# Attention and mixture layers: value products of two key tiles issued together, at steps 3 and 7 of a slot

## What is computed

```
x = x + A(layernorm(x));  x = x + F(layernorm(x))     # twice, A with other weights

A:  q, k = rotary(x Wq), rotary(x Wk);  v = x Wv      # 16 heads of 8
    y = softmax(causal(q k^T * scale)) v;  return y Wp + bp
F:  q, k = x Wq, x Wk                                 # 8 heads of 64, no mask
    v[h] = sum_e gate_v[h, e] * (x Wv[e])             # the two best of 5 experts
    attn = softmax(q k^T / 8) v
    return sum_e mask_o[h, e] * attn[h] Wo[e]         # the two best of 5 experts
```

## Time and profile before

| what | value |
|---|---|
| median of 3 runs | 2078.11 us (2077.97 to 2079.36) |
| the profiled execution's own time | 2074.39 us |
| its span, first to last instruction | 2072.6 us |
| mean granted TensorE clock over the span | 0.967 of full speed |
| busy: TensorE, VectorE, ScalarE, GpSimd | 88%, 76%, 61%, 51% |

### The profile page before, as it was taken

One profiled execution on the slowest core, in us unless ns is written; L12 is line 12 of the kernel. 1 busy time (PEld: TensorE's weight loads), 2 busy tenths in 40 slices (PEclk: granted clock), 3 DMA queues, 4 the chain that ended last, 5 costly groups with the idle time before them and its releaser, 6 DMA issues.

```text
span 2072.6 us, 32651 instructions
## 1 busy us (share of the span) xinstructions
PE 1816.3 (88%) x11328; PEld 881.0 (43%) x11328; DVE 1580.1 (76%) x2934; ACT 1273.3 (61%) x2803; POOL 1047.0 (51%) x1124
## 2 busy tenths in 40 slices
PE   1658999989999898989999998999999899998775
PEld 0223443535444353535444453544435354443332
DVE  4538787888878788788888888887878888787461
ACT  0335757576675757566675756667575766758461
POOL 1223556363645646374655636465563636455433
PEclk8879999999999999999999999999999999999986
DMA  3231203112121302113120211213021121200000
GB/s 97 48 36 32 37 29 43 35 26 30 37 37 42 36 30 33 23 37 36 42 37 30 40 33 27 33 39 37 29 44 35 26 29 37 36 17 14 11 1 6
DMA packets 87617, 68.71 MB, mean 33 GB/s; under 512 B 10720, under 2 KB 83104, under 8 KB 87328
## 3 DMA queue, kind: packets, MB, share of 16 engines
q1 hardware_dynamic: 87456, 66.62, 17.5%
HBM read 32.51 MB, written 10.49 MB: 21 GB/s over the span
## 4 chain that ended last, share of the span: by engine, by line
PE 64%; DVE 13%; ACT 10%; POOL 6%; DMA 3%; issue 3%; SPq 0%; POOLq 0%; DVEq 0%; ACTq 0%; PEldq 0%
PE Y L463 11%; PE M L556 5%; POOL Z L1069 5%; PE S2a L428 5%; ACT Pq L683 5%; PE S1c L404 5%; PE S2b L428 4%; DVE nmaxF L848 4%; PE M L593 3%; PE S1b L404 3%; PE M L514 3%; PE M L489 3%; DMA Ks<-parts 3%; DVE ztmp L930 3%; PE Y L454 2%
## 5 line engine op out<-in xcount | busy, mean ns | idle before, releaser
L1069 POOL TENSOR_TENSOR Z<-Z,ztmp 128x1280 f32<-128x1280 f32 x112 | 324.5, 2897 | 327.9 <-DVE ztmp L958 326.8
L1036 POOL TENSOR_SCALAR_AFFINE_SELECT PT<-PT 128x256 f32<-128x256 f32 (+1 forms) x640 | 254.5, 409 | 386.6 <-ACT PT L668 383.5
L1060 POOL TENSOR_TENSOR Vf<-Vf,ztmp 128x512 f32<-128x512 f32 x256 | 349.0, 1363 | 102.2 <-DVE ztmp L930 93.6
L668 ACT ACTIVATE PT<-S2a 128x512 f32<-128x512 f32 x320 | 191.6, 599 | 170.6 <-PE S2a L422 166.2
L463 PE MATMUL Y<-PT,Vf 128*64 128x512 f32 x1024 | 274.8, 617 | 0.0
L672 ACT ACTIVATE PT<-S2a 128x512 f32<-128x512 f32 x256 | 153.6, 600 | 158.5 <-PE S2a L428 155.7
L930 DVE TENSOR_TENSOR ztmp<-xv,wv_s 128x512 f32<-128x512 f32 x256 | 238.0, 930 | 2.8 <-POOL Z L1069 2.8
L404 PE MATMUL S1c<-Kf,Qf 64*128 64x512 f32 x352 | 203.6, 659 | 36.2 <-ACT Pq L683 32.2
L404 PE MATMUL S1a<-Kf,Qf 64*128 64x512 f32 x352 | 204.5, 662 | 20.6 <-ACT Pq L683 20.6
L668 ACT ACTIVATE PT<-S2b 128x512 f32<-128x512 f32 x320 | 191.5, 598 | 26.3 <-PE S2b L422 26.0
L404 PE MATMUL S1b<-Kf,Qf 64*128 64x512 f32 x320 | 182.8, 652 | 9.5 <-ACT Pq L683 9.5
(11 more groups left out here) (108 smaller groups left out, 3760.7 us busy)
## 6 DMA issues: line engine op xcount, KB each, us to landing
Qs<-parts SPq DMA_DIRECT2D x96, 128.0 KB
Ks<-parts SPq DMA_DIRECT2D x96, 128.0 KB
tab_s<-in_tab SPq DMA_DIRECT2D x16, 512.0 KB, 4.5
xr<-out_x SPq DMA_DIRECT2D x32, 256.0 KB, 2.9
out_x<-res SPq DMA_DIRECT2D x32, 256.0 KB, 2.2
wa_s<-in_wa SPq DMA_DIRECT2D x16, 320.0 KB, 3.1
xl<-out_x SPq DMA_DIRECT2D x16, 256.0 KB, 3.0
out_x<-in_x SPq DMA_DIRECT2D x8, 256.0 KB, 4.4
```

The source lines that it names most:

```text
L668: nc.scalar.activation(PT[:, slot % 2, b, :], t[:, :], ACT.Exp, scale=SCALE_A).then_inc(exps_done.sem, 1)
L1036: last = nc.gpsimd.affine_select(out=v, in_=v, compare_op=ALU.is_ge, fill=0.0, base=0, pattern=pattern, channel_multiplier=-1)
L1060: nc.gpsimd.tensor_tensor(Vf[:, i, :, :], Vf[:, i, :, :], vtmp[:, n % VBUF, :, :], ALU.add).then_inc(v_acc.sem, 1)
L1069: nc.gpsimd.tensor_tensor(Z[:, :, :, :], Z[:, :, :, :], ztmp[:, hh % 2, :, :, :], ALU.add).then_inc(z_acc.sem, 1)
```

## The change

The value products of kt 0 and 1 are both issued at step 3, those of kt 2 and 3 both at step 7; steps 1 and 5 issue none. Nothing else differs: the same instructions, in another place of TensorE's order.

```diff
                         if b < N_BANKS[slot]:
                             pass2(slot, b)
-                        if b % 2 == 1 and b < 2 * NT:
+                        if b in (3, 7):
+                            values(slot, b // 2 - 1)
                             values(slot, b // 2)
                         at = (slot, b)
```

## The result

The change made the kernel slower: a median of 2089.74 us (5 runs, 2089.01 to 2095.52) against 2079.15 us (5 runs of the kernel before, 2077.97 to 2080.10). The ratio is 1.0057, 95% interval 1.0042 to 1.0072, so +10.6 us in the medians. The profiled execution took 2089.01 us; the profiled one of before had 2074.39, which is low among its kind, so the times of the two profiled executions differ by 14.6.

The account below looks back on a forecast made before the run. TensorE bounds most of the span, elsewhere VectorE and GpSimd or the score-bank loop. Offsets sum to +0.20 us an iteration, +3.2 over 16, plus about 1.5 in the last iterations: +4.7, median about 2082.5, range 2064 to 2097.

Parts of the forecast that it names:

- The price of a pair: Any paired value products: the first F tile costs 1.01 us, the further one 0.86, saving 0.15 to 0.25.
- third rival: Seven pairs on the path: a pair saves nothing, 1.05 us more an iteration, +17, total 2099; chance 0.05.
- Slot 0: Step 7's score bank starts where it did, TensorE idles for what it saved, the pair ends later: +0.84 us.
- Slots 1 and 2: Z wait of 1.33 us swallows the rest of the delay; offsets -0.65 at 2.2, -0.05 at 2.4, then +0.37.
- second rival: Step 2.2 scores: the 0.84 isn't swallowed, up to +0.9 us an iteration, +14 on the forecast, 2097; chance 0.17.
- my terms (0.86 less 0.15): Steps 2.2 to 2.4: step 3 gives back 0.86 us, a 0.15 wait for ScalarE takes a part; -0.05 at 2.4.
- Slot 4: Step 1's removal gains nothing; step 3 costs +0.63 us, offset +0.36; steps 5 to 7 change nothing.
- the loop: Slots 2 to 5: score bank, reduction, exponential, next score bank set the pace; no change at slot 4's steps 5 to 7.
- Slots 5 to 7: Offsets +0.40, then -0.5 and -0.45 us around slot 5, -0.23 after slot 6, +0.20 after slot 7.
- first rival: Steps 6.5 and 7.6: banks don't hold TensorE up as VectorE is earlier; -0.9 us an iteration, 2064; chance 0.20.
- The check I had set: Full iteration: forecast wrong if shorter than 118.3 or longer than 119.6 us, or if TensorE's Z wait falls away.
- The total: Whole kernel: +4.7 us, 2074.39 becomes 2079.1 for an execution like the profiled one; median about 2082.5.

Follow-up runs that it names:

- one pair: Kernel before with only key tiles 2 and 3 of slot 0 paired at step 7: ratio 1.0039, iteration 119.67 us.
- the first four experiments: Against the kernel before, pairs only in slots 1-4: 1.0002; only in 0, 5, 6, 7: 1.0053; only tiles 0 and 1: 1.0009; only tiles 2 and 3: 1.0010.

## Why the prediction was right in direction and short in size

- **The price of a pair** was right. Forecast 1.87 us for F (1.01 + 0.86), measured 893.49 to 895.36, 1.87. The rule of the Trainium skill (TensorE: Matmul & The Clock Gate, Part 2: What happens when you issue a matmul) that weights load behind the running matmul, read as "a switch costs nothing", would have given 2.02. The trace disagrees with that here as in the earlier trace rows, and the third rival falls with it.
- **Slot 0**: right, +0.83 for +0.84, and shown alone by one pair. The wait ahead of it was 1.05 us. I said some 0.7, though the 1.1 us that the removed product frees, and a bank that starts where it did, should have given me about 1.
- **Slots 1 and 2**: the total was near (-0.76 for -0.65 at 2.2), but the reason was only partly right. The rest of slot 0's delay is not swallowed by the 1.33 us wait; 0.62 of it survives in the full change, and all of it where A isn't paired. A's pairs at steps 1.3 and 2.3 pay for it. The second rival, that the 0.84 isn't swallowed, described the kernel with F's pairs alone, and in the full change it was true for three quarters. From 2.2 to 2.4 my terms (0.86 less 0.15) give +0.06 and not the -0.05 that I wrote; the trace has -0.31, mainly since TensorE had waited 0.34 us for ScalarE there (at 909.34), and not 0.15.
- **Slot 4** is the step that failed. "Steps 5 to 7 change nothing, the loop decides": the +0.63 at 4.4 was right (VectorE's idle time grew by 0.63), but I carried VectorE's work behind it at its old durations. The products of 0.97, 1.15 and 1.16 us were not fixed prices: each contained a wait for GpSimd. When VectorE came 0.62 us later against GpSimd, they took 1.56, 1.37 and 1.37. That is 0.55 us at step 5.0 and, through the exponentials, 0.42 more by 5.4.
- **Slots 5 to 7**: differences right. -0.91 before 5.6 (I gave 0.9), the wait of the gate product 0.56 and of the projection 0.50 (I gave 0.5 each), +0.32 and +0.63 for the slots (I gave +0.22 from 6.1 on, and +0.43). The first rival, that those waits fall away, didn't happen.
- **The check I had set**, that an iteration of over 119.6 us would prove me wrong, came true with 119.94: the balance per iteration was +0.20 and is +1.15.
- **The total** missed by less than that, and this was luck. Between the two traces lie 2.1 us up to the third iteration, 11.8 in the next fourteen (thirteen full ones and one without an output) and 0.7 behind them. In the kernel before, three of the full iterations took 120.19 to 120.38 us with TensorE's clock at half for a stretch, 4.6 us in all; in the changed kernel none did. Without these the traces would differ by some 19 us, where the forecast had 4.7. I had no term for the clock.
- **The median of the kernel before** lies some 4 us above its profiled execution, and this goes with the clock. Of its 29 runs beside the first four experiments, the four with a mean granted clock of 0.961 have a median of 2080.6 us, the twelve with 0.964 one of 2078.0, and the three with 0.967 or 0.968 one of 2071.7. The profiled execution had 0.967. The changed kernel's five runs had 0.966 to 0.969. What makes the clock fall more often in one run than in the next remains open.

## What to carry to other kernels

When a block of work is moved in one engine's order, ask for each place it leaves what would hold the engine there without it: at step 0.5 the product had been free cover for a wait, and taking it away gained nothing while its copy two steps later cost 0.86 us. The same move can be worth -0.5 us in one slot and +0.87 in another, so try it slot by slot. And a duration read from a busy timeline may contain a neighbour's wait: if instructions of one kind and size show 0.68 us in one place and 1.15 in another, the sum needs both as bounds.

## What was not expected of the hardware

VectorE's product with two operands in SBUF took 0.68 us alone and up to 1.56 us beside an addition on GpSimd, and in the pairs of lines shown it ended 0.54 or 0.55 us after that addition. In the kernel before, the addition grew too, from 1.27 to 1.72. The Trainium skill (SBUF — State Buffer, SBUF: two separate sides) says that the two engines share a pair of ports under an exclusive lock, which a VectorE instruction with two inputs in SBUF needs against a GpSimd instruction that reads SBUF; whichever starts first keeps it to its end and the other is blocked. The runs nearly agree: the two are not slowed in proportion, they run one behind the other. But a product that has waited ends 0.54 to 0.56 us after GpSimd's instruction, and not the 0.68 that it takes alone. That the order of the starts decides who pays was read from the lines, not tried by itself; that the addition stretches the products was tried.

The clock of TensorE fell to half (1.2 GHz) now and then in the middle of the kernel before: three times in its profile, twice some 23 us into an iteration, behind the 1.33 us wait for Z of step 1.9. The first line is the stretch of one such fall, the second the same step in the changed kernel. The columns are the window, its length, the busy time of TensorE, its weight load, VectorE, ScalarE and GpSimd (each with its number of instructions), the granted clock, the DMA's share and its GB/s:

```profile
1255.00:1259.00 4.00, 3.70 (x12) 1.62 (x13) 3.97 (x10) 1.52 (x4) 2.47 (x5) 0.57 0.00 0
```

```profile
907.00:911.00 4.00, 3.62 (x24) 2.27 (x24) 4.00 (x11) 2.81 (x6) 2.78 (x7) 1.00 0.00 0
```

Such an iteration lasted 120.37 us instead of 118.79; in the other full iterations of the same trace the same wait did not lower the clock. Between 280 and 1900 us the four profiles with a wait of 1.33 us at that step had 3, 1, 2 and 1 falls, five of the seven at this step. The five with a wait of 0.42 had none, and the four with 0.83 to 0.90 had two, neither of them at this step. That is suggestive and no more: no run changed the wait alone.
